# Three batches in each round of the engines' loops, in a two-layer graph attention kernel

## The chip, the core and the metric

The kernel runs on one core of one Trainium2 chip. A core has five engines that run their own instruction streams at the same time: TensorE (PE in the profile; PEld is its loading of weights), VectorE (DVE), ScalarE (ACT), GpSimd (POOL) and SyncE (SP), which here only starts transfers. They meet through semaphores: an instruction waits until a count has been reached, and adds to one when it ends. The metric is the device time of one execution, in microseconds (us).

## What is computed

For each of 32 graphs with 256 nodes and 256 features: a graph attention layer with one head (A), a residual and a layer norm; then a layer with 4 heads of 128 (B) and, behind an ELU, one with one head of 256 (C), again a residual and a layer norm. An attention layer in short:

```python
xl = (x @ W).reshape(B, N, H, F)
asrc = jnp.einsum('bnhf,hf->bnh', xl, a_src)
adst = jnp.einsum('bnhf,hf->bnh', xl, a_dst)
e = jax.nn.leaky_relu(asrc[:, :, None, :] + adst[:, None, :, :], NEG_SLOPE)
e = jnp.where(mask[..., None], e, NEG_INF)
attn = jax.nn.softmax(e, axis=1)
out = jnp.einsum('bsdh,bshf->bdhf', attn, xl)
...
x = _layernorm(x + _L0_gnn_ref(x, adj, ...), axis=-1)
x = _layernorm(x + _L1_gnn_ref(adj, x, ...), axis=-1)
```

## The kernel before

A batch is one graph. Its work is cut into five stages, and in turn `i` every engine works on five batches at once: stage 0 of batch `i` (t0), stage 1 of batch `i-1` (t1), and so on to stage 4 of batch `i-4` (t4). Stages 0 and 1 are layer A and its norm, stage 2 is layer B, stages 3 and 4 are layer C and the last norm. The order of the work in a turn is written out by hand, one list for each engine (its `body`). A helper in the list waits for its semaphores and issues its instructions; `Turn` gives the counts to wait for.

The names that matter below, all in one turn. On PE, `project_b` (L821) multiplies into VectorE's input four times, the last time for `(0, 1)` into bank 0; `spread(B, 0)` and `spread(B, 1)` (L847) transpose score columns of `VB`, with `transpose_weights(A)` (L858) between them. On DVE the list begins with `norm_last(1, 5, t4)` (L698, writes `y2`) and `values_b(0, 1, 0, t2)` (L677, writes the part of `VB` that `spread(B, 1)` reads), and it ends with `norm_last(0, 3, t3)` (L698), `inverse_sum(C, 1, 5, t3)` (L642) and `values_b(1, 0, 4, t2)` (L677). `low_b` (L663) comes once in a turn. SP's `load_adj` and `load_xT` start the loads of the next batch at the head of its list.

`iterations` runs each engine's list: turns 0 to 4 written out (constants as counts), then a loop of its own on each engine over turns 5 to 31, then turns 32 to 35 written out. In the loop the counts hang on the turn, so the head of each pass computes them into registers: for six offsets the turn plus the offset, and for six more the same times 16, since a transfer adds 16. The built program packs several of these steps into one instruction. No barrier stands between the engines at the loop's end; each branches back by itself.

Counted in the built program with its waits, a pass of the loop has 149 instructions on DVE, 272 on PE, 72 on ACT, 43 on POOL and some 22 on SP. DVE has run 483 instructions of its list before the loop.

Of the kernel before, what the change touches and what calls it, by code (L numbers as in the profile page):

```python
# [14 lines left out]
DMA = 16  # L15
# [34 lines left out]
        return self.counts is not None or self.at > 0  # L50


COUNTS = [(k, 1) for k in range(-4, 2)]
DMA_COUNTS = [(k, DMA) for k in range(-4, 2)]


def gat_kernel(nc, x, xT, adj, adjT, w0, a0, w1, asrc1, adst1, b1, w2, asrc2, adst2, b2, out):
# [10 lines left out]
    NB, N, D = x.shape  # L68
# [9 lines left out]
    with ctx:  # L78
# [130 lines left out]
                    return  # L209

        def iterations(eng, body, needed):
            LAG = 4
            for i in range(LAG + 1):
                body(Turn(i))
            regs = {(k, step): eng.alloc_register(f"count{k + LAG + 1}x{step}") for k, step in needed}
            with eng.Fori(LAG + 1, NB) as i:
                counts = {}
                for k, step in needed:
                    r = regs[(k, step)]
                    eng.reg_add(r, i, k)  # L220
                    if step > 1:
                        eng.reg_mul(r, r, step)
                    counts[(k, step)] = eng.snap(r, min_val=(LAG + 1 + k) * step, max_val=(NB + k) * step)
                body(Turn(i, counts))
            for i in range(NB, NB + LAG):
                body(Turn(i))

# [9 lines left out]
        def _(sp):  # L237
# [55 lines left out]
            sp.dma_start(A.W[:, :, 0, 2:D + 2], w0.rearrange("(k p) f -> p k f", p=P)).then_inc(A.s_wld, DMA)  # L293
            sp.dma_start(att0[:, :], a0.rearrange("f o -> (f o)").partition_broadcast(P)).then_inc(A.s_wld, DMA)
            iterations(sp, body, COUNTS + DMA_COUNTS)
            sp.wait_ge(s_out, DMA * NB)

        @block.gpsimd
        def _(pool):
# [81 lines left out]
            def body(i):  # L381
# [12 lines left out]
                diagonal(t1)  # L394

            iterations(pool, body, COUNTS + DMA_COUNTS)

        @block.scalar
        def _(act):
# [114 lines left out]
            act.wait_ge(s_cst2, 1)  # L514
            act.wait_ge(s_b1, 1)
            iterations(act, body, COUNTS + DMA_COUNTS)

        @block.vector
        def _(dve):
            def score_columns(L, heads):  # L520
                dve.wait_ge(L.s_wld, L.loads * DMA)
                n_ab = 2 * L.KT * heads[0]
                for h in heads:
                    for k in range(L.KT):
                        for j in range(2):
                            if L is A:
                                v = att0[:, (1 - j) * D:(2 - j) * D]
                            elif L is B:
                                v = att1[:, j, h * L.F:(h + 1) * L.F]
                            else:  # L530
                                v = att2[:, j, :]
                            nc.vector.scalar_tensor_tensor(out=prod[:, j, 0:L.F], in0=L.W[:, k, h, 2:L.F + 2],
                                                           scalar=0.8 if j == 0 else -0.8, in1=v, op0=ALU.mult,
                                                           op1=ALU.mult, accum_out=L.W[:, k, h, j:j + 1])\
                                .then_inc(L.s_wab, 1)
                            n_ab += 1
                            if n_ab > 1:
                                dve.wait_ge(L.s_wab, n_ab - 1)
                dve.wait_ge(L.s_wab, n_ab)
# [244 lines left out]
            score_columns(B, (0, 1))  # L784
            iterations(dve, body, COUNTS + DMA_COUNTS)

        @block.tensor
        def _(pe):
# [133 lines left out]

            iterations(pe, body, COUNTS + DMA_COUNTS)

# [26 lines left out]
```

## Time and profile before

| | |
|---|---|
| median of 3 runs | 738.02 us (737.86 to 738.05) |
| the profiled execution | 738.62 us, of which the core's span is 736.9 us |
| PE busy | 661.6 us (90% of the span) |
| DVE busy | 600.0 us (81%) |
| ACT, POOL busy | 437.5 us (59%), 371.1 us (50%) |
| granted TensorE clock | 0.977 of full speed on average, full in the loop |

The span runs from the first to the last instruction of the core. Busy time leaves out register, branch, semaphore and transfer-starting instructions, so a stretch in which an engine only handles those shows as idle. "issue" as the cause of an idle time means that the profile shows nothing that the engine waited for.

### The profile page before, as it was taken

The page shows a single profiled execution, that of the slowest core. Times are in us where ns is not written, and L with a number is a line of the kernel's source. Part 1 is how long each engine was busy: PE and PEld are TensorE (multiplying, and loading weights), DVE is VectorE, ACT ScalarE, POOL GpSimd, SP SyncE. Part 2 cuts the span into 40 slices and gives each one's busy share as a digit, 9 for nine tenths or more (in the row PEclk, how much of TensorE's full clock was granted, in tenths as well). Part 3 has the DMA queues.
Part 4 walks back from the last instruction along what each step waited for, and adds up shares of the span by engine and source line. Part 5 has one row for each costly group of instructions (what it writes and reads, how often), then busy time and mean ns, then how long its engine had stood idle before and what let it go on. Part 6 is the DMA issues. An engine that isn't in the chain of part 4 may idle for free. (4 is left out here: it accounts for less than half of the span.)

```text
span 736.9 us, 17753 instructions
## 1 busy us (share of the span) xinstructions
PE 661.6 (90%) x3848; PEld 567.6 (77%) x3848; DVE 600.0 (81%) x2367; ACT 437.5 (59%) x1154; POOL 371.1 (50%) x746
## 2 busy tenths in 40 slices
PE   2469999999999999999999999999999999999973
PEld 1358888888888887888888888888888888888762
DVE  2567888898888898988888989888889888888862
ACT  1235667666555676655557766555677665556651
POOL 0214456555555565545555655555566555555542
PEclk9679999999999999999999999999999999999997
DMA  7201221222222212222222122122221221221110
GB/s 211 67 21 59 80 89 56 78 93 69 81 93 93 78 64 79 93 64 85 93 93 75 57 89 93 61 88 93 93 61 67 93 91 59 93 93 64 40 45 32
DMA packets 56002, 57.49 MB, mean 78 GB/s; under 512 B 3760, under 2 KB 51504, under 8 KB 55984
## 3 DMA queue, kind: packets, MB, share of 16 engines
q1 hardware_dynamic: 53152, 55.06, 23.2%
q10 hardware_dynamic: 2832, 2.23, 1.0%
q8 instruction: 6, 0.10, 0.1%
q14 instruction: 12, 0.10, 0.0%
HBM read 36.31 MB, written 8.39 MB: 61 GB/s over the span
## 5 line engine op out<-in xcount | busy, mean ns | idle before, releaser
L437 ACT ACTIVATE probB<-probB,shiftB 128x256 f32<-128x256 f32 x256 | 127.6, 505 | 86.3 <-DVE probB L632 85.9
L367 POOL TENSOR_SCALAR probB<-probB,rdenB 128x256 f32<-128x256 f32 x256 | 119.0, 477 | 59.8 <-DVE rdenB L649 57.6
L877 PE MATMUL PS<-probTB,VB 128*128 128x256 f32 x512 | 132.1, 380 | 1.1 <-ACT probTB L448 0.9
L359 POOL TENSOR_TENSOR x1b<-x,b2p 128x512 f32<-128x512 f32 x32 | 40.8, 1274 | 171.6 <-DMA x1c<-x1b 163.5
L834 PE MATMUL PS<-WC,hidT 128*128 128x258 f32 x512 | 122.1, 381 | 2.1 <-DVE probB L632 1.4
L632 DVE SCALAR_TENSOR_TENSOR probB<-PS,VB,gatedB 128x256 f32<-128x256 f32 x256 | 108.8, 477 | 0.8
L834 PEld LDWEIGHTS PS<-WC,hidT 128*128 128x128 f32 x512 | 94.7, 190 | 15.4 <-DVE probB L632 1.7
L877 PEld LDWEIGHTS PS<-probTB,VB 128*128 128x128 f32 x512 | 92.1, 190 | 12.7 <-ACT probTB L448 1.7
L590 DVE CUSTOM_DVE_ANT_0 gatedB<-PS,gateB 128x256 f32<-128x256 f32 x256 | 95.6, 420 | 5.3 <-PE PS L847 0.7
L808 PE MATMUL PS<-WA,xTin 128*128 128x258 f32 x256 | 70.0, 399 | 12.0 <-DMA xTin<-in_x_t_dram 12.0
L448 ACT ACTIVATE probTB<-PS 128x512 f32<-128x512 f32 x128 | 76.7, 600 | 4.5 <-PE PS L858 0.9
L821 PE MATMUL PS<-WhB,inhB 128*128 128x260 f32 x256 | 75.8, 296 | 2.1 <-DVE inlB L663 2.1
L858 PE MATMUL PS<-ident,probB 128*128 128x128 f32 x512 | 74.2, 276 | 3.4 <-POOL probB L367 3.4
L821 PE MATMUL PS<-WlB,inhB 128*128 128x260 f32 x256 | 73.5, 287 | 0.0
L821 PE MATMUL PS<-WhB,inlB 128*128 128x260 f32 x256 | 73.4, 287 | 0.0
L448 ACT ACTIVATE probTA<-PS 128x512 f32<-128x512 f32 x32 | 19.1, 597 | 90.1 <-PE PS L858 90.1
L858 PEld LDWEIGHTS PS<-ident,probB 128*128 128x128 f32 x512 | 60.3, 141 | 13.6 <-issue 5.0
L866 PE MATMUL PS<-VC,probTC 128*128 128x257 f32 x256 | 69.8, 397 | 0.8 <-ACT probTC L448 0.8
L677 DVE TENSOR_TENSOR VB<-PS,b1x 128x260 f32<-128x260 f32 x128 | 53.5, 418 | 13.4 <-PE PS L821 13.2
L866 PE MATMUL PS<-VA,probTA 128*128 128x257 f32 x256 | 62.6, 388 | 1.0 <-ACT probTA L448 1.0
L808 PEld LDWEIGHTS PS<-WA,xTin 128*128 128x128 f32 x256 | 47.2, 201 | 20.0 <-issue 12.0
L866 PEld LDWEIGHTS PS<-VC,probTC 128*128 128x128 f32 x256 | 47.3, 194 | 13.2 <-issue 7.6
(90 smaller groups left out, 1363.6 us busy)
## 6 DMA issues: line engine op xcount, KB each, us to landing
adj_in<-in_adj_dram SPq DMA_DIRECT2D x32, 256.0 KB, 2.8
xTin<-in_x_t_dram SPq DMA_DIRECT2D x32, 256.0 KB, 3.0
xres<-in_x_dram SPq DMA_DIRECT2D x32, 256.0 KB, 3.0
adjT_in<-in_adj_t_dram SPq DMA_DIRECT2D x32, 256.0 KB, 2.8
x1c<-x1b SPq DMA_DIRECT2D x32, 256.0 KB, 2.3
out_dram<-res SPq DMA_DIRECT2D x32, 256.0 KB, 2.2
gateC<-gateB SPq DMA_DIRECT2D x32, 128.0 KB, 2.0
WB<-in_L_gnn_W_dram ACTq DMA_DIRECT2D x2, 256.0 KB, 6.0
```

Of the source, the lines that this page charges most:

```text
L367: last = pool.tensor_scalar(B.prob[h][:, k, :], B.prob[h][:, k, :], B.rden[:, k, h:h + 1], 1.0, ALU.mult, ALU.mult)
L437: last = nc.scalar.activation(L.prob[h][:, k, :], L.prob[h][:, k, :], ACT.Exp, bias=L.shift[:, k, h:h + 1], accum_out=den[:, k, h:h + 1] i ...
L448: nc.scalar.activation(L.probT[h][:, :, :], PS[b][:, :].rearrange("p (k n) -> p k n", k=NT), ACT.Copy)\
L590: last = nc.vector.tensor_tensor_reduce(out=L.gated[h][:, k, :], in0=PS[b][:, (h % 2) * N:(h % 2 + 1) * N], in1=L.gate[:, k, :], scale=0.2 ...
L632: last = nc.vector.scalar_tensor_tensor(out=L.prob[h][:, k, :], in0=PS[b][:, (h % 2) * N:(h % 2 + 1) * N], scalar=L.V[:, k, h, 1:2], in1=L ...
L677: nc.vector.tensor_tensor(B.V[:, tile, hs, :], PS[b][:, 0:2 * (B.F + 2)].rearrange("p (h f) -> p h f", h=2), b1x[:, hs, :], ALU.add).then_ ...
L808: last = nc.tensor.matmul(PS[b][:, 0:D + 2], xTin[:, k, tile * P:(tile + 1) * P], A.W[:, k, 0, :], start=(k == 0), stop=(k == A.KT - 1))
L821: last = nc.tensor.matmul(PS[b][:, 0:2 * (B.F + 2)], x_[:, k, tile * P:(tile + 1) * P], w_[:, k, 2 * g:2 * (g + 1), :].rearrange("p h f -> ...
L834: last = nc.tensor.matmul(PS[b][:, 0:D + 2], hidT[:, k, tile * P:(tile + 1) * P], C.W[:, k, 0, :], start=(k == 0), stop=(k == C.KT - 1))
L858: last = nc.tensor.transpose(PS[b][:, o:o + P], L.prob[h][:, q, k * P:(k + 1) * P], ident[:, :])
L866: last = nc.tensor.matmul(PS[b][:, 0:L.F + 1], L.probT[0][:, k, u * P:(u + 1) * P], L.V[:, k, 0, 2:L.F + 3], start=(k == 0), stop=(k == NT ...
L877: last = nc.tensor.matmul(PS[b][:, o:o + N], B.V[:, k, h, 2:B.F + 2], B.probT[h][:, k, :], start=(k == 0), stop=(k == NT - 1))
```

## The change

The loop now runs over rounds of three turns: (32 - 5) / 3 = 9 rounds in place of 27 passes. The counts are computed once a round, as round times 3 (or 48) plus a constant, and for eight offsets in place of six, since the second and third turn of a round reach two further. The list of each engine stands three times in the loop. The turns ahead of the loop and behind it are as they were, and so is the order of the work on each engine.

```diff
-COUNTS = [(k, 1) for k in range(-4, 2)]
-DMA_COUNTS = [(k, DMA) for k in range(-4, 2)]
+COUNTS = [(k, 1) for k in range(-4, 4)]
+DMA_COUNTS = [(k, DMA) for k in range(-4, 4)]
...
-            LAG = 4
+            LAG, TURNS = 4, 3
             for i in range(LAG + 1):
                 body(Turn(i))
             regs = {(k, step): eng.alloc_register(f"count{k + LAG + 1}x{step}") for k, step in needed}
-            with eng.Fori(LAG + 1, NB) as i:
+            with eng.Fori(0, (NB - LAG - 1) // TURNS) as i:
                 counts = {}
                 for k, step in needed:
                     r = regs[(k, step)]
-                    eng.reg_add(r, i, k)
-                    if step > 1:
-                        eng.reg_mul(r, r, step)
+                    eng.reg_mul(r, i, TURNS * step)
+                    eng.reg_add(r, r, (LAG + 1 + k) * step)
                     counts[(k, step)] = eng.snap(r, min_val=(LAG + 1 + k) * step, max_val=(NB + k) * step)
-                body(Turn(i, counts))
+                for turn in range(TURNS):
+                    body(Turn(i * TURNS + (LAG + 1), counts, turn))
```

On DVE, the head of the loop before: the packed register instructions (L216 to L222, `ISA`), and behind them the first two of the list.

```order
L216 UNCONDITIONAL_BRANCH
L216 ISA
L220 ISA x2
L222 ISA
L698 SCALAR_TENSOR_TENSOR y2<-PS5,rdenC,x1c 128x256
L677 TENSOR_TENSOR VB<-PS0,b1x 128x260
```

Four packed instructions (and a register move that the listing leaves out) stand ahead of the list in every turn. The same place now, once in three turns: seven packed register instructions in place of four.

```order
L216 UNCONDITIONAL_BRANCH
L216 ISA
L220 ISA
L221 ISA
L222 ISA
L220 ISA
L221 ISA
L222 ISA
```

The head has grown by three packed instructions and lost the move; behind it the same list begins.

On DVE, the end of each turn before: the three last of the list, then the count of the loop and the branch back to the head.

```order
L698 SCALAR_TENSOR_TENSOR y2<-PS3,rdenC,x1c 128x256
L642 RECIPROCAL rdenC<-PS5 128x1
L677 TENSOR_TENSOR VB<-PS4,b1x 128x260
L216 REGISTER_ALU
L216 COMPARE_AND_BRANCH
```

This stood behind all turns of the loop. The end of the first and of the second turn of a round now: the next turn's first two follow at once.

```order
L698 SCALAR_TENSOR_TENSOR y2<-PS3,rdenC,x1c 128x256
L642 RECIPROCAL rdenC<-PS5 128x1
L677 TENSOR_TENSOR VB<-PS4,b1x 128x260
L698 SCALAR_TENSOR_TENSOR y2<-PS5,rdenC,x1c 128x256
L677 TENSOR_TENSOR VB<-PS0,b1x 128x260
```

Between these turns neither count, branch nor head is left. Behind the third turn the count and the branch stand as before. Counted as above, a round of the loop has 435 instructions on DVE (7 in its head, 142 in each turn, 2 at its end), 806 on PE, 207 on ACT and some 116 on POOL.

## Rows read from the trace of the kernel before

**Rows 1.** Busy time by engine in ten turns of the loop.
```profile
core 0: us, PE busy (x) PEld busy (x) DVE busy (x) ACT busy (x) POOL busy (x), PEclk, DMA share, GB/s
297.26:508.59 211.33, 201.17 (x1202) 174.31 (x1202) 183.39 (x722) 135.63 (x360) 115.58 (x230) 1.00 0.25 81
```

**Rows 2.** Waits in the same ten turns: us in total, times, longest.
```profile
DVE inlB L663 <- ACT inhB L473: 10.0, 10, 1.0
DVE y L698 <- issue: 9.9, 10, 1.0
...
PE PS L847 <- DVE y L698: 7.1, 10, 0.7
...
PE PS L847 <- ACT VC L427: 3.1, 10, 0.3
DVE VB L677 <- PE PS L821: 2.8, 10, 0.3
```

**Rows 3.** Timeline of DVE across one loop end: start, us, what.
```profile
339.46 0.16 DVE L642 RECIPROCAL rdenC<-PS 128x1 f32<-128x1 f32 x1
339.53 0.41 DVE L677 TENSOR_TENSOR VB<-PS,b1x 128x260 f32<-128x260 f32 x1
340.93 0.48 DVE L698 SCALAR_TENSOR_TENSOR y<-PS,rdenC,x1c 128x256 f32<-128x256 f32 x1 [0.99 <-issue]
341.33 0.41 DVE L677 TENSOR_TENSOR VB<-PS,b1x 128x260 f32<-128x260 f32 x1
```

**Rows 4.** Timeline of PE across the same loop end.
```profile
336.20 1.03 PE L866 MATMUL PS<-VC,probTC 128*128 128x257 f32 x4
337.00 0.36 PE L821 MATMUL PS<-WhB,inhB 128*128 128x260 f32 x1
...
339.84 0.28 PE L821 MATMUL PS<-WhB,inlB 128*128 128x260 f32 x1
340.09 0.62 PE L847 MATMUL PS<-ident,VB 128*128 128x128 f32 x4
340.55 0.60 PE L858 MATMUL PS<-ident,probA 128*128 128x128 f32 x4
341.85 0.62 PE L847 MATMUL PS<-ident,VB 128*128 128x128 f32 x4 [0.70 <-DVE y L698]
```

**Rows 5.** Line L663, once a turn: turns written out, then turns of the loop.
```profile
L663 DVE TENSOR_TENSOR inlB<-PS,inhB x2: 692/692/692, 83.6 to 103.9; 128x512 fp32r<-128x512 f32 x2
L663 DVE TENSOR_TENSOR inlB<-PS,inhB x10: 691/692/692, 315.0 to 505.2; 128x512 fp32r<-128x512 f32 x10
```

**Rows 6.** Transfer queues by stretch: 0 to 121, 122 to 686, 686 to 736.9 us.
```profile
q8 instruction: 4, 0.07, 0.3%
q14 instruction: 7, 0.06, 0.2%
...
q1 hardware_dynamic: 43302, 44.87, 24.5%
...
q8 instruction: 2, 0.03, 0.3%
q14 instruction: 4, 0.03, 0.2%
```

**Rows 7.** The queues in 121 to 122 and in 80.9 to 81.9 us.
```profile
q14 instruction: 1, 0.01, 3.2%
...
q8 instruction: 1, 0.02, 10.6%
```

**Rows 8.** Busy time between two transfers of q8, at 80.94 and at 100.72 us.
```profile
80.94:100.72 19.78, 19.47 (x119) 16.97 (x118) 17.52 (x68) 13.02 (x36) 8.89 (x18) 1.00 0.21 69
```

**Rows 9.** Transfers: KB each, median us from issue to landing.
```profile
xTin<-in_x_t_dram SPq DMA_DIRECT2D x32, 256.0 KB, 3.0
...
gateC<-gateB SPq DMA_DIRECT2D x32, 128.0 KB, 2.0
```

**Rows 10.** Busy share of the transfer engines in 338 to 345 us, 40 slices; SP's issues.
```profile
DMA  0000049998006978799999940049994000000000
...
339.18 0.37 SPq L249 DMA_DIRECT2D adj_in<-in_adj_dram  x1
339.72 0.37 SPq L243 DMA_DIRECT2D xTin<-in_x_t_dram  x1
```

## Prediction

> **What bounds the kernel now.** The busy time by engine in ten turns of the loop comes first. A turn takes 211.33 / 10 = 21.13 us, and PE is busy for 20.12 of them, DVE for 18.34, ACT for 13.56, POOL for 11.56 [rows 1]. So PE's list sets the length of a turn, and what can be won in the loop is at most PE's idle time, 1.02 us a turn. The waits of the same ten turns say where that idle time is: 0.71 us a turn ahead of a transposition of line 847 that waited for DVE, and 0.31 us ahead of one that waited for ACT [rows 2]. DVE's own list has an entry of the same count: 0.99 us a turn ahead of line 698 with "issue" as its cause, so DVE waited for nothing that another engine does [rows 2].
>
> The two timelines show that these belong together. DVE ends its last instruction of a turn at 339.53 + 0.41 = 339.94, and the first of the next, L698, starts at 340.93 [rows 3]: in the 0.99 us between lie the loop's count, its branch and the head's register instructions. L677 follows L698 and ends at 341.74 [rows 3]; it writes the scores that `spread(B, 1)` transposes, and PE, done with the one before at 340.55 + 0.60 = 341.15, starts at 341.85 after 0.70 us of waiting [rows 4]. The wait row names L698, but the instruction that ends last before PE's start is L677. PE's own branch costs it nothing that is seen: its last matmul of a turn starts at 336.20 and runs to 337.23, the next turn's first starts at 337.00 [rows 4].
>
> **What it removes.** 18 of the 27 loop ends. Without one, L698 could start at 339.94. L677 needs PE's last matmul of `project_b(0, 1)`, which ends at 339.84 + 0.28 = 340.12 [rows 4], so it would start right behind L698, at about 340.35, and end at 340.8, ahead of the 341.15 at which PE gets there. PE's wait would be gone: 0.71 us a turn. The trace holds a second price, since the turns ahead of the loop are written out: from one `low_b` to the next, once a turn, it takes 103.9 - 83.6 = 20.3 us there, and (505.2 - 315.0) / 9 = 21.13 us in the loop [rows 5], 0.8 us less. PE does nearly the same work in both; DVE has a little less. I take 0.75 us, between the two: 18 x 0.75 = 13.5 us, with bounds of 12.8 and 14.4. DVE doesn't become the bound: its 18.34 us busy, 1.0 us of waiting for ACT's copy and 0.28 for PE [rows 1, 2] make 19.6, under 20.4.
>
> **What it adds to the head.** DVE's head goes from four packed register instructions and a move to seven. The nearest row is the whole gap of 0.99 us [rows 3]. If all of it were the four, three more would be 0.74 us; if the branch took most of it, near nothing. I take 0.6 us, since the gap hides the part of the work that runs while the last instruction is still busy, so a longer head shows in full. At the head PE is already waiting, so all of it is passed on: 9 x 0.6 = 5.4 us (0 to 6.7). The larger heads of PE, ACT, POOL and SP lie beside other work: PE shows no gap at its branch [rows 4], and ACT and POOL are idle for 7.6 and 9.6 us a turn [rows 1]. Without that cover each would cost what DVE's does.
>
> These terms alone give 738.0 - 13.5 + 5.4 = 729.9 us.
>
> **What it adds in code.** This term decides. Instructions come by transfer, and the queues named "instruction" show it: 18 pieces in all, 11 in the first 121 us, one between 121 and 122, none between 122 and 686 us, where only the data queue has a row, and 6 after that [rows 6, 7]. So in the loop each engine found its whole pass on the core. The pieces are of two sizes: q14's 7 hold 0.06 MB, 8 KB each, and q8's 4 hold 0.07 MB, 16 KB each [rows 6]. Between two of q8, PE runs 119 matmuls and 118 weight loads [rows 8], with 23 waits between them in the program: 260 instructions for 16 KB, some 64 bytes each. A piece of 8 KB is then 128 instructions, and DVE's 149 a pass lie in two or three pieces. They also come early: the one at 121 to 122 us comes when DVE is, by the count of its list, some 585 instructions in, with about 50 left to its first branch back, and no pass needs another after it. So it was a piece further on that was fetched ahead, and the core kept the loop's pieces beside it. Three pieces at least are kept; four or more isn't shown.
>
> A round now has 435 instructions on DVE, 435 / 128 = 3.4 pieces, so it lies in four at least (it starts some 483 instructions in), and with the one fetched ahead that makes five. ACT with 207 and POOL with 116 need two or three, as DVE did. If the core keeps four pieces for DVE, the fifth takes the place of the first, and each branch back finds its target gone: DVE stands still until 8 KB have come from memory. That happens at 8 branches back (the ninth round ends without one). Nothing in the trace has this price. The nearest rows: one piece of 8 KB takes 3.2% of 16 engines in 1 us, 0.5 us of transfer alone [rows 7], which bounds it from below; the smallest transfer in the list, inside the core, lands 2.0 us after its issue, and one that reads memory 3.0 us [rows 9]. I take 3.0, since the fetch reads memory too, and it starts as SP has just issued the loads at 339.18 and 339.72, when most slices of the transfer engines stand at 7 to 9 tenths [rows 10]; for the same reason 4 us is my upper bound. All of it comes ahead of L698, where PE already waits, so it adds to PE's idle time: 8 x 3.0 = 24 us (4 to 32).
>
> [...]
>
> **The sum.** 738.0 - 13.5 + 5.4 + 24 = 753.9, so 754 us. The profiled execution took 738.62 us, 0.6 more than the median; all terms are differences, so I put them on the median of 738.02.
>
> **The rivals.**
>
> *All pieces stay.* If DVE keeps five pieces, or fetching ahead doesn't push out the loop's first, only the first two terms count: 729.9 us, 731.9 with their worse ends (12.8 won, 6.7 lost), 723.6 with the better. For it: no refetch shows in 564 us, and the number of pieces that stay has a lower bound only. Against it: the piece fetched ahead at 121 us shows that the prefetch goes on at a loop's end whether it is needed or not. It decides at 8.1 / 8 = 1.0 us a miss: cheaper ones leave the kernel faster. Chance 0.25.
>
> *PE misses too.* A round of PE has 806 instructions, 806 / 256 = 3.1 pieces of 16 KB, in four of them, five with the one ahead. With room for four PE fetches 16 KB at each branch back as well: 3.0 us plus 0.5 for the second 8 KB. PE runs its list ahead of its array, as the closed seam at 337 us shows [rows 4]; I let 1 us be covered by that, and 8 x 2.5 = 20 us come on top: 774 us. Against it: PE's pieces are twice DVE's, so its memory is probably the larger. [...] Chance 0.11.
>
> *It evens out.* Misses of 0.9 to 1.2 us, or a partly hidden fetch, end within 0.2% of 738.0. The 0.5 us of pure transfer [rows 7] and any latency at all leave little room for just that. Chance 0.03.
>
> **How the numbers follow.** DVE misses alone: 0.61, forecast 754, its own range 744 (2.0 us a miss give 729.9 + 16 = 745.9, a little less with the terms' better ends) to 764 (4 us a miss give 761.9, and 2 more with the worse ends). The rival on the other side holds 0.25, so the range must reach it: 728 to 765 leaves out the case in which PE misses too (0.11), and the edges of the others, some 0.08. A measurement of this kernel can tell 0.2%, 1.5 us, from no change. Faster: 0.25; within: 0.03; slower: the two cases with misses, 0.72.
>
> **What the profile after would show.** Right: q14's instruction pieces spread through the loop, 16 or more beyond today's 12, two at least a round; "issue" ahead of L698 in nine entries, eight of them around 0.99 + 0.6 + 3.0 = 4.6 us, and no such entry in the other 18 turns; a round of 3 x 20.4 + 0.7 + 0.6 + 3.0 = 65.5 us in place of 63.4; PE's wait at L847 only once a round. Wrong by the first rival: no instruction pieces in the loop, gaps of 1.6 us, a round of 62.5. The second: q8 pieces in the loop and PE idle at the round's first matmul (L821). The forecast fails if the fetch is far cheaper than a load, or if more stays on the core than the four pieces that I assume; the first-turn price is wrong if a turn without a loop end doesn't come down to 20.4 us.

## The result

The changed kernel takes 766.2 us (763.1 to 766.5), the kernel before 738.0: a ratio of 1.037, with an interval of 1.0345 to 1.0399. It is slower, as forecast, but by 28.2 us where 16 were forecast, and 1 us outside the range. The profiled execution took 766.52 us, of which 764.2 are the span, against 738.62 and 736.9 before.

The page of the changed kernel has three lines to put beside the ones of before: the granted clock in 40 slices, and the queues that bring instructions.

```profile
PEclk9979999998998999999899999989999998999996
...
q14 instruction: 56, 0.46, 0.2%
q8 instruction: 8, 0.13, 0.1%
```

There were 12 pieces of q14 and 6 of q8. The clock line shows an 8 again and again in the loop, where the kernel before has nines only. The waits (us in total, times, longest):

```profile
DVE y L698 <- issue: 36.7, 9, 4.8
...
PE PS L847 <- DVE y L698: 34.2, 9, 4.6
```

The gap ahead of L698 is now there 9 times and not 27, but lasts up to 4.8 us, and nearly all of it shows as waiting of PE. Ten turns of before had 9.9 us of it [rows 2], so 27 had 26.7. In one round, 238.23 to 305.75 us, the queues are:

```profile
q1 hardware_dynamic: 4937, 5.11, 23.5%
q14 instruction: 5, 0.04, 0.2%
```

Five pieces of 8 KB are fetched in this round, and none of q8. The timeline of VectorE across one branch back answers to [rows 3]:

```profile
371.81 0.41 DVE L677 TENSOR_TENSOR VB<-PS,b1x 128x260 f32<-128x260 f32 x1
377.06 0.48 DVE L698 SCALAR_TENSOR_TENSOR y<-PS,rdenC,x1c 128x256 f32<-128x256 f32 x1 [4.84 <-issue]
```

And TensorE at the same place answers to [rows 4]; below it, the busy time by engine in pieces of 2 us from 374 on (the last three columns are the granted clock, the transfer engines' share and GB/s).

```profile
372.37 0.62 PE L847 MATMUL PS<-ident,VB 128*128 128x128 f32 x4
372.83 0.60 PE L858 MATMUL PS<-ident,probA 128*128 128x128 f32 x4
377.98 1.09 PE L847 MATMUL PS<-ident,VB 128*128 128x128 f32 x4 [4.55 <-DVE y L698]
378.86 3.65 PE L834 MATMUL PS<-WC,hidT 128*128 128x258 f32 x8
```

```profile
374.00:376.00 2.00, 0.00 (x0) 0.00 (x0) 0.00 (x0) 0.06 (x1) 0.00 (x0) 1.00 0.43 144
376.00:378.00 2.00, 0.02 (x1) 0.05 (x1) 0.94 (x3) 0.00 (x0) 0.00 (x0) 0.51 0.01 4
378.00:380.00 2.00, 2.00 (x7) 1.81 (x8) 1.90 (x11) 0.00 (x0) 0.00 (x0) 0.50 0.35 131
380.00:382.00 2.00, 2.00 (x6) 1.53 (x6) 1.67 (x5) 1.41 (x6) 1.28 (x1) 0.50 0.00 0
382.00:384.00 2.00, 2.00 (x9) 1.68 (x8) 0.25 (x2) 0.81 (x5) 0.00 (x0) 0.78 0.00 0
384.00:386.00 2.00, 2.00 (x11) 1.74 (x10) 2.00 (x12) 1.45 (x3) 1.83 (x4) 1.00 0.00 0
```

This is what the prediction didn't have. TensorE has stood still since 372.83 + 0.60 = 373.43, and from 376 on its clock is granted at about 0.50 of full speed. The engine has work again at 377.98, but the clock comes back only between 382 and 384. The eight passes of L834 take 3.65 us there; at the full clock they take 1.91 us. A round of the loop takes 67.52 us (238.23 to 305.75) or 66.05 us (the next), where the prediction had 65.5, with a mean granted clock of 0.95 or 0.97 in it:

```profile
238.23:305.75 67.52, 62.78 (x362) 54.48 (x362) 55.07 (x218) 40.91 (x108) 34.70 (x69) 0.95 0.24 76
305.75:371.80 66.05, 61.60 (x363) 53.65 (x362) 55.07 (x218) 40.91 (x108) 34.72 (x69) 0.97 0.25 78
```

VectorE does the same work in both, PE is busy for 1.2 us longer in the first.

### The profile page after: what moved, and what is told of

It is laid out like the page before. It is cut to its first block and busy times, and to the rows that moved or that the text cites. A ratio compares the mean times of both kernels' runs of the same rounds, so it can differ in the third digit from the quotient of the medians.

```text
span 764.2 us, 17294 instructions
## 1 busy us (share of the span) xinstructions
PE 674.5 (88%) x3848; PEld 580.3 (76%) x3848; DVE 601.1 (79%) x2367; ACT 439.3 (57%) x1154; POOL 371.3 (49%) x746
## 3 DMA queue, kind: packets, MB, share of 16 engines
q1 hardware_dynamic: 53152, 55.06, 22.5%
## 5 line engine op out<-in xcount | busy, mean ns | idle before, releaser
L834 PE MATMUL PS<-WC,hidT 128*128 128x258 f32 x512 | 134.1, 409 | 2.1 <-DVE probB L632 1.4
L834 PEld LDWEIGHTS PS<-WC,hidT 128*128 128x128 f32 x512 | 103.0, 207 | 18.3 <-DVE probB L632 1.7
L847 PE MATMUL PS<-ident,VB 128*128 128x128 f32 x256 | 43.1, 295 | 34.7 <-DVE y L698 34.2
L821 PE MATMUL PS<-WhB,inlB 128*128 128x260 f32 x256 | 73.4, 287 | 0.0
L866 PE MATMUL PS<-VA,probTA 128*128 128x257 f32 x256 | 64.2, 395 | 1.0 <-ACT probTA L448 1.0
```

The costliest lines, as they stand in the source:

```text
L821: last = nc.tensor.matmul(PS[b][:, 0:2 * (B.F + 2)], x_[:, k, tile * P:(tile + 1) * P], w_[:, k, 2 * g:2 * (g + 1), :].rearrange("p h f -> ...
L834: last = nc.tensor.matmul(PS[b][:, 0:D + 2], hidT[:, k, tile * P:(tile + 1) * P], C.W[:, k, 0, :], start=(k == 0), stop=(k == C.KT - 1))
L866: last = nc.tensor.matmul(PS[b][:, 0:L.F + 1], L.probT[0][:, k, u * P:(u + 1) * P], L.V[:, k, 0, 2:L.F + 3], start=(k == 0), stop=(k == NT ...
```

## The experiments

Theory A: VectorE's code no longer stays on the core, so each of its 8 branches back waits for a fetch; TensorE waits with it, and its clock falls. Theory B: the loss is the price of more code or longer heads on all engines. All runs were timed in three rounds against the kernel before on the same chip.

### e1: name the branch back at the head of VectorE's loop

```diff
-            with eng.Fori(0, (NB - LAG - 1) // TURNS) as i:
+            with nc.Fori(0, (NB - LAG - 1) // TURNS, engines=bass.OrderedEngineSet([eng.engine]),
+                         hint_back_edge=eng is nc.vector) as i:
```

The rest is the changed kernel, with three turns a round. The edit puts one more instruction at the head of VectorE's loop, which the trace calls BRANCH_PREFETCH_HINT (39 ns, once a round).

> [...] Theory A (VectorE's branch back waits for its code; the 3.5 us there make TensorE idle for over 4 us, after which its clock is granted at half for 3 to 7 us): both losses go, a round takes 3 x 20.32 + 0.8 + 0.6 = 62.4 us in place of 66.8, the time is 729 to 732 us, the issue gap ahead of L698 is 1.6 to 1.8 us and the granted clock in the loop is full. Theory B (the loss comes from what all engines carry now, larger code on TensorE or larger heads, not from VectorE's target): 760 us or more, as the changed kernel.

Measured: 732.2 us, ratio 0.991 (0.9891 to 0.9935), at the upper end of what theory A gave. Its waits (a line more in the file, so L699 and L848 are the L698 and L847 of above) and its queues between 180 and 640 us:

```profile
DVE y L699 <- issue: 14.2, 9, 1.7
...
PE PS L848 <- DVE y L699: 11.6, 9, 1.4
```

```profile
q1 hardware_dynamic: 36256, 37.50, 25.3%
```

One instruction on VectorE turns the loss of 28 us into a gain of 6. No piece is fetched between 180 and 640 us, not even ahead of time, and the clock there is full (1.00). Behind VectorE's branch back at 232.4 us the head's first register instruction starts at 232.7; in the changed kernel the branch stands at 238.2 and this instruction at 241.4. The longest gap is 1.7 us, about the predicted length of a head without a miss. Theory B falls: TensorE's larger code and all heads are still there.

The fetches are not all gone. Behind the loop, 6 us after its last branch, VectorE stands once for 2.0 us in the middle of straight code, as an instruction piece comes (675.7 us), and TensorE's clock is at half (0.50 in 680 to 682 us) for 3.4 us behind it. The waits of 660 to 700 us:

```profile
DVE amaxB L591 <- issue: 2.0, 1, 2.0
```

So in the loop the piece behind it was no longer fetched ahead; this fits a room of four pieces, which is enough for a loop that touches four when nothing is fetched beyond it. No run isolates it.

### e2 and e3: three turns on VectorE alone, and on all but VectorE

```diff
-            LAG, TURNS = 4, 3
+            LAG, TURNS = 4, 3 if eng is nc.vector else 1
```

> Three turns a round on VectorE alone; the other four engines keep one turn a round. Theory A: as the changed kernel, 766 us within 3, with gaps of 4.8 us ahead of L698 and a half clock behind them. Theory B: what the other engines add is gone, so most of the loss is too: under 750 us.

Measured: 775.2 us, ratio 1.049 (1.0472 to 1.0512). VectorE's longer loop alone brings the loss, as theory A says, but it is 9 us larger than in the changed kernel, and I had allowed 3. Its gaps are longer (row below; 36.7 in the changed kernel), and each of its 8 low stretches of the clock in the loop lasts 6.8 us, where in the changed kernel five last 6.8 and three 3.4. My estimate from the two traces: the gaps are 4.6 us longer in all, and TensorE works for some 44 us at half clock in place of 35, which costs up to 4.7 us more. That is the size of the 9 us; why both are longer stays open.

```profile
DVE y L698 <- issue: 41.3, 9, 5.2
```

For all but VectorE the edit is `1 if eng is nc.vector else 3`.

> Three turns a round on all engines but VectorE, which keeps one turn a round (its counts now by a product and a sum, some 0.1 us more a turn). Theory A: 738 to 741 us, no gap over 1.3 us ahead of L698, full clock in the loop. If TensorE's 806 instructions a round also had to be fetched again: q8 pieces in the loop and 750 us or more.

Measured: 743.9 us, ratio 1.007 (1.005 to 1.0089), 3 us over what I expected. No fetch between 180 and 640 us, q8 included (e10 shows that q8 brings TensorE's code), so TensorE's 806 instructions stay on the core: the rival "PE misses too" is out. The gap of VectorE has grown through the product and sum of each count, from 0.99 to 1.17 us a turn (31.7 / 27), and a turn from 21.13 to 21.33 us (low_b, 211.2 to 616.5 us in 19 turns):

```profile
DVE y L698 <- issue: 31.7, 27, 1.2
...
PE PS L847 <- DVE y L698: 24.1, 27, 1.0
...
L663 DVE TENSOR_TENSOR inlB<-PS,inhB x20: 691/692/692, 211.2 to 616.5; 128x512 fp32r<-128x512 f32 x20
```

27 x 0.2 = 5.4 us, which is the measured loss of 5.4. A longer head on VectorE shows in full.

### e4 and e5: two turns a round, and the same code 68 instructions further on

```diff
-            LAG, TURNS = 4, 3
+            LAG, TURNS = 4, 2
...
-            for i in range(NB, NB + LAG):
+            for i in range(NB - (NB - LAG - 1) % TURNS, NB + LAG):
```

> Two turns a round (13 rounds, turn 31 written out behind the loop). VectorE's loop has 293 instructions and lies in three pieces of 128, four with the one fetched ahead. Theory A with room for four pieces: no fetch in the loop, 14 loop ends less (14 x 0.81 = 11.3 us won), 13 heads with two or three packed instructions more (13 x 0.4 = 5.2 us lost): 732 us within 2. [...]

Measured: 732.0 us, ratio 0.991 (0.9893 to 0.993). No instruction piece between 180 and 640 us. (The two lists of offsets are one shorter too.)

e5 is e4 with 68 small instructions on VectorE, once, ahead of everything:

```diff
+            for k in range(68):
+                nc.vector.memset(pad[:, k:k + 1], 0.0)
             nc.vector.memset(minus1[:, :], -1.0).then_inc(s_b1, 1)
```

> The kernel with two turns a round and, on VectorE alone, 68 one-column memsets of an unused tile at its very start, where it waits for a load anyway (they cost 4 us at most, once). The loop's 293 instructions are the same, but now begin some 551 instructions in and end at 844, so that they touch four pieces of 128 in place of three, five with the one fetched ahead. Theory A (room for four pieces, the fifth replaces the first): 12 branches back wait 3.5 us each and the half clock comes on top: 732 + 12 x 5 = 792 us, 780 to 805, with q14 pieces all through the loop. Rival (what counts is the size of the loop, 293 instructions against a memory for 512, or the number of turns written out): 732 to 737 us, no pieces in the loop.

Measured: 793.0 us, ratio 1.074 (1.0723 to 1.0765). Its waits, and its queues between 180 and 640 us:

```profile
DVE y L699 <- issue: 54.1, 13, 5.0
```

```profile
q1 hardware_dynamic: 32000, 33.04, 22.6%
q14 instruction: 49, 0.40, 0.3%
```

The loop is the same, instruction by instruction; only its place has changed. The time goes from 732 to 793 us. The memsets themselves cost nothing that is seen: the first `low_b` starts at 38.4 us, against 38.5 in e4. So neither the size of the loop (293 instructions, 18.8 KB by the estimate of 64 bytes each; the 512 of the rival are four pieces of 128) nor the number of turns decides, but where it lies.

That it lay in three pieces of 128 instructions before and lies in four now doesn't follow from my counts alone, since the list's first instruction need not begin a piece: with pieces counted from there, 483 to 776 would be four pieces and 551 to 844 three. The times at which the pieces come settle it. Ahead of the loop of e5 VectorE's come at 73.4, 93.5, 111.8 and 130.7 us, when it has 327, 454, 584 and 713 instructions behind it in the trace, waits included: one piece for every 128 or so. The kernel before has the same places (453 at 102.3 us, 585 at 121.1). Behind a branch back (336.3 us) they come at 337.6, 340.2, 343.7, 364.9 and 383.0 us, the last three 34, 164 and 289 instructions on, which from 551 are the places 585, 715 and 840. So a piece is fetched when VectorE comes to the end of another, and the boundaries lie near 454, 582, 710 and 838. The loop of e4, 483 to 776, lies in three pieces; that of e5, 551 to 844, in four, by some 6 instructions; that of the changed kernel, 483 to 918, in four.

So three pieces and the one ahead stay, four and the one ahead don't. The 49 pieces in 460 us are some 5 in each round of 47 us, as in the changed kernel: once there is one piece too many, all of them are fetched anew in every round, not the first alone.

### e6, e7 and e8: move the transposition that waits

```diff
+                project_c(0, 6, t3)
                 spread(B, 1, 5, t2)
-                project_c(0, 6, t3)
```

> The kernel before with one row of TensorE's list moved: the second transposition of layer B's scores stands behind the first projection of layer C (1.9 us of matmuls) in place of ahead of it. Theory A (TensorE's 0.7 us wait a turn is VectorE's loop end, passed on through this transposition): TensorE has other work there, the wait goes, and VectorE's list with its gap of 0.99 us becomes the bound near 20.6 us a turn: 719 to 727 us. Rival (some other chain of the turn takes over at once): within 2 us of 738.

Measured: 737.9 us, ratio 1.000 (0.9987 to 1.0007). I was wrong and the rival right. The wait ahead of L847 for L698 is gone, but in ten turns PE waits as follows:

```profile
PE PS L847 <- ACT VC L427: 3.1, 10, 0.3
PE PS L858 <- POOL probB L367: 2.7, 10, 0.3
PE PS L834 <- issue: 2.4, 10, 0.2
```

and a turn is as long as before. The last two rows are new. The middle one names a second path: the scores of layer B, which VectorE starts right behind its loop end, go through ACT's exponentials and POOL's scaling back to TensorE. VectorE's gap lies on both paths, and the second must have been hidden behind the first by less than the 0.7 us. That is read from the names in the row; no run isolates it. So "PE waits for 0.7 us at L847" was a true row, and its removal still worth nothing.

e7 moves the transposition behind two more rows (`weigh(A, 0)`, `weigh(A, 1)`) in the changed kernel.

> The changed kernel (three turns a round, the fetch at VectorE's branch back unchanged) with the same transposition moved behind 3.8 us of TensorE's other matmuls, so that TensorE works through most of VectorE's stall. Theory A with the clock: VectorE's stall stays at 4.8 us and now bounds the round, but TensorE's clock doesn't fall; the round is 60.5 + 4.8 = 65 us or a little more in place of 66.8: 748 to 754 us, granted clock full in the loop. Rival (the 1.3 us a round beyond the stall is no matter of the clock): the low clock stays, 760 us or more.

Measured: 759.8 us, ratio 1.030 (1.0275 to 1.0323), 6 us over what I expected and just under what the rival gave. Inconclusive on the clock: TensorE now stops at its next wait for VectorE, the second projection of layer C, and its clock still falls in seven of the eight rounds, for 3.4 us in five of them and 6.8 in two.

```profile
DVE y L698 <- issue: 35.8, 9, 4.8
PE PS L834 <- DVE probB L632: 24.3, 9, 2.8
```

e8 is e4 with the move of e6.

> Two turns a round as in the run before this call, with the transposition moved as in e6. If both gains add up: 14 turns lose the loop end of VectorE too, so VectorE needs 20.0 us in them and TensorE 20.3: 717 to 722 us. If the move has taken all that the loop end cost: as e6, within 2 us.

Measured: 732.0 us, ratio 0.991 (0.9884 to 0.993), as e4, which neither of my two cases had: the move adds nothing here either, and takes nothing away.

### e9: add work so that TensorE's clock stays

```diff
+            def keep_busy(b, t):
+                bank_free(pe, b, A.s_norm[0], t)
+                for _ in range(8):
+                    nc.tensor.matmul(PS[b][:, 0:D + 2], ones[:, :], C.W[:, 0, 0, :], start=True, stop=True)
...
+                if i.counts is not None and i.off == 0:
+                    keep_busy(1, t1)
                 spread(B, 1, 5, t2)
```

> The changed kernel with work added: in the first turn of each round TensorE runs eight more 128x258 matmuls of constants into a bank that is free then, right ahead of the transposition that waits for VectorE. By the row of such matmuls (0.24 us a pass, two passes each) they take 3.8 us and lie inside TensorE's 4.2 to 4.6 us of waiting; their result is not used. Theory A with the clock (the 1.3 us a round beyond the stall is TensorE's clock falling to half after its wait): the clock stays full, eight rounds lose 1.6 us less, the first round 2.5 us more: 753 to 758 us, with 4.8 us gaps on VectorE as before. Rival (the clock doesn't hang on this wait, or something else makes up the difference): 766 us or more, since work was only added.

Measured: 752.0 us, ratio 1.018 (1.0166 to 1.02), 1 us under what I expected. With 72 useless matmuls more the changed kernel is 14 us faster. VectorE's gaps are 1.4 us shorter in all than without them, and the clock line of the page has only nines in the loop:

```profile
PEclk9979999999999999999999999999999999999996
...
DVE y L698 <- issue: 35.3, 9, 4.5
...
PE PS L852 <- DVE y L698: 3.6, 7, 0.7
```

The fetches are all still there, 56 pieces of q14. The eight matmuls of the first turn of a round stand in the trace as 16 passes (L804 at 238.51 us), 3.65 us in all. The turns with a stall, from `low_b` to `low_b`, take 24.4 us on average, against 26.2 in the changed kernel: 1.8 us for each of the eight, 14.2 in all. At most 1.4 us of that can be the shorter gaps; the rest goes with the clock. This is the missing term, isolated.

### e10 and e11: no loop at all

```diff
+            if UNROLLED(eng):
+                for i in range(NB + LAG):
+                    body(Turn(i))
+                return
```

`UNROLLED` is true for all engines in e10, for VectorE alone in e11.

> No loop: all 36 turns of every engine written out with constants as counts. Theory A: what costs is a branch back whose target is gone, not the amount of code; straight code is fetched ahead. No heads, no loop ends: 27 turns of 20.32 in place of 21.13, 738.0 - 21.9 = 716 us within 2, with instruction pieces all through the span and no issue gap ahead of L698. Rival (fetching much more code costs by itself, by late pieces or by the transfer engines' time): 725 us or more.

Measured: 718.7 us, ratio 0.974 (0.9722 to 0.9754), the fastest of all; 0.7 us above the expected band. Its queues between 180 and 640 us:

```profile
q8 instruction: 23, 0.38, 0.3%
q14 instruction: 44, 0.36, 0.2%
```

67 pieces come in 460 us, where the changed kernel has 34. The 23 of q8, none of which comes in these 460 us where TensorE runs a loop, bring TensorE's code: 22.5 turns of at most 806 / 3 = 269 instructions are some 260 to a piece. There is no issue gap ahead of `norm_last` any more. The turns are no longer alike: about half take 20.32 us, the others up to 21.8, 20.47 on average. So straight code is fetched ahead, and what it costs is at most the 0.15 us by which the average turn is over 20.32. What costs is the jump to a target that is gone.

> Only VectorE's list is written out; the other engines keep the loop of the kernel before. Theory A (only VectorE's loop end is on the path that sets a turn's length): as with all written out, 716 us within 2. Rival (a loop end of another engine takes over once VectorE's is gone): 720 to 735 us.

Measured: 720.7 us, ratio 0.976 (0.974 to 0.9773). That is 2.7 us over theory A's band, at the lower edge of the rival's, and 2.0 us over e10: these 2 us may be the loop ends of the other four engines. 17.5 of the 19.5 us that all loop ends together cost go with VectorE's alone. Between 180 and 640 us 25 pieces come, all of q14 (0.20 MB): 22.4 turns of VectorE's 142 instructions are 127 to a piece of 8 KB, the 128 and the 64 bytes of the prediction.

## Why the prediction was right in kind and off in size

**What bounds the kernel, and the two prices of a loop end.** Right. Turns without a loop end take 20.32 us in the changed kernel, in the middle of each round, against 21.13: 0.81 us each, the upper of the two prices. 18 x 0.81 = 14.6 us won, where 13.5 were taken and 14.4 was the bound. But the reason that I gave for the lower price, PE's wait of 0.7 us at L847, was not the whole: e6 took this wait away and won nothing. The written-out turns of the trace [rows 5] carried the whole effect, and the single wait row would not have.

**The longer head.** 0.6 us taken. The turn across the loop's entry, which has a head and no miss, went from 20.87 us in the kernel before (low_b at 103.9 and 124.8 us) to 21.42 in the changed one (104.9 and 126.3): 0.55 us, 9 x 0.55 = 4.9 us lost. e3 shows the same coupling with 0.2 us a turn.

**The fetch.** Right in place, number and nearly in price: 8 branches back; nine gaps stand in the trace, and the one at the loop's entry, 1.3 us, has no fetch. The gaps sum to 36.7 us; nine of 1.5 us (0.99 + 0.55, my estimate of a head without a miss) are 13.9, which leaves 22.8 us for eight fetches, 2.9 us each where 3.0 were taken from the loads. One fetch stands in the trace itself: 3.2 us from VectorE's branch back at 238.2 us to the head's first register instruction at 241.4, where the kernel before has 0.3 (191.6 to 191.9), 2.9 us more. That the fetch reads memory, the reason for taking 3.0, was my assumption; the runs show its price, not its source. No row of before shows the room for four pieces on which these 8 fetches rest: "four pieces and the one ahead don't fit" was an assumption. e4, in three pieces, fetched none between 180 and 640 us, and e5, in four, 49. I gave two pieces a round as the least; it is five. The rivals "all pieces stay" and "PE misses too" are out, by the page after and by e3.

**What failed.** The step "it adds to PE's idle time: 8 x 3.0 = 24 us". It held the idle time to be the whole price of a stall. In each of the eight stalls TensorE's clock had fallen to half (0.50) by the time the engine got work again, and the engine then ran on at half speed, in the stall shown for 5 us (377.98 to 382.9). The terms as measured are 738.0 - 14.6 + 4.9 + 22.8 = 751.1 us. e9, with the clock kept up, lands within 1 us of that: 752.0, less the 1.8 us by which the added matmuls lengthen the first round, where no stall hides them. The eight turns with a stall are 14.2 us longer in all in the changed kernel than in e9, 1.8 us each, nearly all of it the clock's. 751.1 + 14.2 = 765.3, of the 766.2 measured. The trace of before held the sign of it: its clock of 0.977 over the span with a full clock in the loop [rows 1] means a low clock at the start and at the end, where TensorE waits often: it is 0.50 in 20 to 30 us, 0.67 in 30 to 40 and 0.66 in 720 to 730, and TensorE is busy for 7.2, 3.3 and 5.3 us of these 10. I read the column as harmless, since it said 1.00 where the change acts, and did not ask what a stall of 4.5 us would do to it.

**The room for code.** VectorE kept four pieces of 8 KB, one of them fetched ahead, and not five (e4, e5). With one more, five were fetched in each round (5 of q14 in 238.23 to 305.75 us).

**The clock.** The granted clock of the 2 us windows above is 0.50 for the first matmuls behind the stall. In this stall TensorE had stood still for 2.6 us (373.43 to 376.0) when the clock fell, and had worked for 4.9 us (377.98 to 382.9) when it was granted in full again; over the eight stalls it fell 2.0 to 3.8 us after TensorE's last matmul had ended.

Open: why the low stretch lasts 6.8 us in some rounds and 3.4 in others, why e2's gaps are longer, and whether e1's added instruction works by leaving out the fetch ahead.

## What to carry to other kernels

Before a loop's body is made longer, count its instructions on each engine, waits included, and the places where they begin and end: what mattered here is how many fetch pieces the body touches. One more than fits made each branch back wait for code, 2.9 us here, and 68 instructions far ahead of the loop decided it. With the branch back named at the loop's head (e1) that cost was down to one wait of 2.0 us behind the loop, and in straight code to 0.15 us a turn at most. And when a change makes TensorE wait for several us, price the wait twice: the idle time (up to 4.6 us here), and the time at half clock behind it (which cost up to 1.8 us a stall here); compare with turns of the same trace that lack the wait, not with the one wait row alone, since a second path may lie right behind it.

## What the hardware showed that I had not expected

- VectorE's loop keeps three pieces of 128 instructions and one ahead (e4); with four and one ahead five pieces are fetched in each round (e5: 49 in 460 us). One piece too many has the whole set fetched anew, though the long wait is at the branch alone.
- The place of a loop in the code alone is worth 61 us of 732 (e4, e5).
- With the branch back named at the loop's head, no piece is fetched between 180 and 640 us, though the loop touches four, and VectorE waits for one once behind the loop, 2.0 us (e1).
- Useless matmuls in a wait make the kernel faster: 766.2 to 752.0 us (e9).
